# Three products of rounded halves for four readouts, output work shared with two more engines, and new orders on every queue

## The reference

```python
xn = layernorm(x)
scores = einsum('bsd,bmd->bsm', xn, ctx) / sqrt(256)
scores = where(mask, scores, -1e30)
x = x + where(any(mask), softmax(scores) @ ctx, 0)
y = layernorm(x)
h = square(relu(quant_act(y) @ quant_weight(w1).T))      # 8-bit rows, ternary weights
out = x + quant_act(h) @ quant_weight(w2).T
# quant_act: row scaled by 127/max|row| (max at least 1e-5), rounded, scaled back
# quant_weight: gamma = mean|w| + 1e-5; clip(round(w/gamma), -1, 1) * gamma
```

## Time and profile before

| | us |
|---|---|
| median of 3 runs | 66.76 |
| runs | 65.42, 67.02, 66.76 |
| the profiled execution, own time | 65.26 |
| its span, first to last instruction | 63.5 |
| TensorE busy | 59.2 (93%) |
| VectorE, ScalarE, GpSimd busy | 46.3, 46.0, 35.9 |

### The profile page before, as it was taken

The page is one execution under the profiler, slowest core; times in us unless marked ns, Lnnn a source line. Parts: engine busy times, 40 slices in busy tenths (PEclk is TensorE's granted clock), DMA queues, the critical chain, the costliest instruction groups (busy, mean ns, idle before and its releaser), DMA issues.

```text
span 63.5 us, 1281 instructions
## 1 busy us (share of the span) xinstructions
PE 59.2 (93%) x345; PEld 44.0 (69%) x345; DVE 46.3 (73%) x158; ACT 46.0 (72%) x89; POOL 35.9 (57%) x91
## 2 busy tenths in 40 slices
PE   5999999999999999999999999999999799989930
PEld 1337589499898888888958767858687285769710
DVE  0335463995379783595978989899799999999540
ACT  1624937999979799999995693889795799760300
POOL 4340319459002897685738988883898776840000
PEclk9999999999999999999999999999999999999999
DMA  0899999999200010188021647926482718222522
GB/s 0 218 329 312 361 372 401 408 399 404 101 0 0 10 40 7 24 164 148 5 41 41 127 80 151 168 40 134 96 165 51 155 45 163 88 83 83 170 82 88
DMA packets 15024, 9.13 MB, mean 144 GB/s; under 512 B 11557, under 2 KB 13865, under 8 KB 15017
## 3 DMA queue, kind: packets, MB, share of 16 engines
q1 hardware_dynamic: 15008, 9.05, 53.6%
q10 hardware_dynamic: 8, 0.00, 0.0%
HBM read 5.24 MB, written 1.05 MB: 99 GB/s over the span
## 4 chain that ended last, share of the span: by engine, by line
PE 89%; POOL 2%; DVE 2%; issue 1%; ACT 1%; DVEq 0%; POOLq 0%
PE ps_v L389 22%; PE ps_sp L368 13%; PE ps_h L419 9%; PE ps_o L459 6%; PE ps_sp L378 6%; PE ps_h L291 5%; PE ps_h L305 3%; PE ps_sp L350 3%; PE ps_v L459 3%; PE ps_h L368 3%; PE ps_o L327 2%; POOL q L1145 2%; PE ps_sp L419 2%; PE ps_sp L297 2%; PE ps_in L340 1%; PE ps_in L327 1%
## 5 line engine op out<-in xcount | busy, mean ns | idle before, releaser
L389 PE MATMUL ps_v<-ctx_sb,probs_T 128*128 128x256 f32 x64 | 15.3, 383 | 0.0
L389 PEld LDWEIGHTS ps_v<-ctx_sb,probs_T 128*128 128x128 f32 x64 | 11.7, 190 | 2.2 <-issue 0.3
L859 DVE TENSOR_SCALAR_CACHE_REDUCE hidden<-ps_h 128x1024 f32<-128x1024 f32 x6 | 7.3, 1215 | 0.4 <-PE ps_h L419 0.3
L419 PE MATMUL ps_h<-w_T,q_T 128*128 128x512 bf16 x28 | 7.2, 380 | 0.0
L808 DVE CUSTOM_DVE_ANT_0 neg_s<-ps_sp,mask_bias 128x512 f32<-128x512 f32 x7 | 4.8, 689 | 3.0 <-PE ps_sp L368 2.3
L1061 POOL TENSOR_SCALAR ln_ve<-ln_mv 128x2 f32<-128x2 f32 (+1 forms) x5 | 1.0, 194 | 10.1 <-DVE ln_mv L770 10.1
L629 ACT ACTIVATE dev<-x,x_sum 128x256 f32<-128x256 f32 x8 | 4.0, 503 | 3.2 <-DVE x L820 3.2
L616 ACT ACTIVATE probs<-neg_s,neg_max 128x513 f32<-128x513 f32 x8 | 5.7, 716 | 0.3 <-DVE neg_max L808 0.3
L649 ACT ACTIVATE q_i<-hidden,qscale 128x1024 int16<-128x1024 f32 x5 | 5.7, 1138 | 0.0
L368 PE MATMUL ps_sp<-ctx_T_hi,xn_T_hi 128*128 128x512 f32 x12 | 5.3, 444 | 0.0
L820 DVE SCALAR_TENSOR_TENSOR x<-ps_v,recip_sum,x_sb 128x256 f32<-128x256 f32 x8 | 3.9, 482 | 2.0 <-PE ps_v L389 1.9
(11 more groups left out here) (136 smaller groups left out, 147.1 us busy)
## 6 DMA issues: line engine op xcount, KB each, us to landing
ctx_sb<-in_ctx_dram SPq DMA_DIRECT2D x4, 512.0 KB, 7.2
w_sb<-in_L_ffn_w_dram SPq DMA_DIRECT2D x2, 512.0 KB, 6.9
w_sb<-in_L_ffn_w_dram SPq DMA_DIRECT2D x1, 1024.0 KB, 8.5
out_dram<-x_sb SPq DMA_DIRECT2D x8, 128.0 KB, 1.7
x_sb<-in_x_dram SPq DMA_DIRECT2D x3, 256.0 KB, 7.5
x_sb<-in_x_dram SPq DMA_DIRECT2D x2, 128.0 KB, 3.0
q_Ti<-q_i SPq DMA_TRANSPOSE x11, 3.0
w_T<-w_int SPq DMA_TRANSPOSE x4, 3.3
```

The lines of the kernel that those rows point to most:

```text
L389: last = nc.tensor.matmul(ps_v[:, 0:D], probs_T[:, t % 2, c * P:(c + 1) * P], ctx_sb[:, t // TB, c, :], start=(c == 0), stop=(c == MC - 1))
L419: last = nc.tensor.matmul(h_bank(t)[:, n * FH:(n + 1) * FH], q1_T[:, t, dc, :], w1_T[:, n * (FC // 2):(n + 1) * (FC // 2), dc, :], start=( ...
L859: nc.vector.tensor_scalar(hidden[:, t % 3], h_bank(t)[:, :], 0.0, 0.0, ALU.min, ALU.min, accum_out=hidden_min[:, t:t + 1]).then_inc(hidden ...
```

## The change

- Tiles 2 to 5 (batches 1 and 2): `readout` becomes `readout_high` (8 matmuls: rounded probabilities by rounded context, rounded probabilities by context remainder) and `readout_low` (4 matmuls: remainder of the probabilities by rounded context), all float32r, 256 columns, with the next tile's `prob_transposes` between the two. `ctx_rows_high` (ScalarE, one instruction of 128x1024 for each batch) and `ctx_rows_low` (GpSimd, the same size) make the context's halves; `probs_low` (VectorE, 128x512 from PSUM, four times) makes the remainder of the probabilities.
- `weight_integers` moves from GpSimd to VectorE; `cast_q2` of tiles 0 to 2 moves from VectorE to GpSimd; the output step of tiles 0 to 4 is split into a scaling copy on ScalarE (`output_scaled`) and an addition on GpSimd (`output_added`).
- The mask's spread contracts 128 rows of which 124 are zero, where it had four; a memset on VectorE clears them.
- The order of the calls is new on every engine. The number of constant products in the middle is ten, where it was eight.

```diff
+
+HALVED = (1, 3)
+
+CAST = 3
+
...
+        pick = sbuf("pick", [P, B, P], bf16)
+        mask_rows = sbuf("mask_rows", [P, M], bf16)
         mask_bias = sbuf("mask_bias", [P, B, M], f32)
 
...
+        ctx_lo = sbuf("ctx_lo", [P, HALVED[1] - HALVED[0], MC, D], f32r)
         x1 = sbuf("x1", [P, T, D], f32)
 
         x1_sum = sbuf("x1_sum", [P, T], f32)
...
@@ -153,6 +164,7 @@
         ctx_in = [sem(f"ctx_in{b}") for b in range(B)]
...
                 sp.wait_ge(q2i_done, t + 1)
-                if t >= 2:
-                    sp.wait_ge(q2_cast, t - 1)
+                if 2 <= t < CAST + 2:
+                    sp.wait_ge(q2_cast_pool, t - 1)
+                elif t >= 2:
+                    sp.wait_ge(q2_cast, t - 1 - CAST)
                 sp.dma_start_transpose(q2_Ti[:, t % 2], q2_i[:, t % 2]).then_inc(q2_turned[t % 2], 16)
 
             def store(t):
                 b, i = divmod(t, TB)
-                sp.wait_ge(out_ready, t + 1)
+                if t < SHARED:
+                    sp.wait_ge(out_added, t + 1)
+                else:
+                    sp.wait_ge(out_ready, t - SHARED + 1)
...
@@ -259,22 +280,22 @@
             load_ctx(2)
             load_x(3)
             load_ctx(3)
+            turn_weight(0, 0)
             turn_q1(0)
-            turn_weight(0, 0)
             turn_weight(0, 1)
             turn_q1(1)
             turn_q1(2)
+            turn_q2(0)
+            turn_q1(3)
             turn_weight(1, 0)
-            turn_q1(3)
+            turn_q2(1)
+            turn_q1(4)
             turn_weight(1, 1)
-            turn_q2(0)
-            turn_q1(4)
-            turn_q2(1)
             turn_q1(5)
             turn_q2(2)
             turn_q2(3)
+            turn_q2(4)
             store(0)
-            turn_q2(4)
             store(1)
             store(2)
...
                     pe.wait_ge(bias_done, 2)
+                elif halved(t - 1):
+                    pe.wait_ge(plo_done, t - TB * HALVED[0])
                 else:
...
+                last.then_inc(v_done, 1)
+
+            def readout_high(t):
+                b = t // TB - HALVED[0]
+                pe.wait_ge(p_copied, t + 1)
+                pe.wait_ge(ctxlo_done, b + 1)
+                pe.wait_ge(x1_done, t)
+                for part in (ctx_hi, ctx_lo):
+                    for c in range(MC):
+                        nc.tensor.matmul(ps_v[:, 0:D], probs_T_hi[:, t % 2, c * P:(c + 1) * P], part[:, b, c, :],
+                                         start=(part is ctx_hi and c == 0), stop=False)
+
+            def readout_low(t):
+                pe.wait_ge(plo_done, t - TB * HALVED[0] + 1)
+                for c in range(MC):
+                    last = nc.tensor.matmul(ps_v[:, 0:D], probs_T_lo[:, t % 2, c * P:(c + 1) * P],
+                                            ctx_hi[:, t // TB - HALVED[0], c, :], start=False, stop=(c == MC - 1))
                 last.then_inc(v_done, 1)
...
-                if t < TURNED:
-                    pe.wait_ge(q2_cast, t + 1)
+                if t < CAST:
+                    pe.wait_ge(q2_cast_pool, t + 1)
+                elif t < TURNED:
+                    pe.wait_ge(q2_cast, t + 1 - CAST)
                 else:
...
+                elif t - 2 < SHARED:
+                    pe.wait_ge(o_scaled, t - 1)
                 else:
-                    pe.wait_ge(out_ready, t - 1)
+                    pe.wait_ge(out_ready, t - 2 - SHARED + 1)
...
             first_scores(1)
             ctx_transposes(1, 1)
             scores(1)
+            warm_up(ps_q, 128, 4)
             prob_transposes(0)
             x_transposes(1)
-            warm_up(ps_q, 128, 5)
+            warm_up(ps_q, 128, 3)
             weight_sum(0)
             warm_up(ps_q, 128, 3)
             readout(0)
             scores(2)
             ctx_transposes(2, 0)
+            x_transposes(2)
+            prob_transposes(1)
             ctx_transposes(2, 1)
-            prob_transposes(1)
+            scores(3)
+            readout(1)
+            prob_transposes(2)
+            ctx_transposes(3, 0)
+            scores(4)
             weight_sum(1)
-            scores(3)
-            x_transposes(2)
-            prob_transposes(2)
-            readout(1)
-            ctx_transposes(3, 0)
+            readout_high(2)
             prob_transposes(3)
-            scores(4)
+            readout_low(2)
             ctx_transposes(3, 1)
-            readout(2)
+            scores(5)
             x_transposes(3)
-            scores(5)
+            hidden_product(0)
+            readout_high(3)
             prob_transposes(4)
-            readout(3)
-            hidden_product(0)
-            readout(4)
+            readout_low(3)
+            scores(6)
+            readout_high(4)
             prob_transposes(5)
-            scores(6)
+            readout_low(4)
             hidden_product(1)
-            readout(5)
+            readout_high(5)
+            prob_transposes(6)
+            readout_low(5)
+            scores(7)
             hidden_product(2)
-            prob_transposes(6)
-            scores(7)
-            hidden_product(3)
             readout(6)
             prob_transposes(7)
+            hidden_product(3)
+            readout(7)
             hidden_product(4)
-            readout(7)
+            q1_transposes(6)
             output_product(0)
             hidden_product(5)
-            q1_transposes(6)
             hidden_product(6)
+            q1_transposes(7)
             output_product(1)
-            q1_transposes(7)
+            hidden_product_half(0)
             output_product(2)
-            hidden_product_half(0)
             hidden_product_half(1)
+            output_product(3)
             q2_transposes(5)
-            output_product(3)
+            output_product(4)
             q2_transposes(6)
-            output_product(4)
             output_product(5)
             q2_transposes_half(0)
             output_product(6)
...
+            def ctx_rows_high(b):
+                act.wait_ge(ctx_in[b], 16)
+                nc.scalar.activation(ctx_hi[:, b - HALVED[0]], ctx_sb[:, b], ACT.Copy).then_inc(ctxhi_done, 1)
+
...
-                nc.scalar.activation(probs_T[:, t % 2], ps_p, ACT.Copy).then_inc(p_copied, 1)
+                nc.scalar.activation((probs_T_hi if halved(t) else probs_T)[:, t % 2], ps_p, ACT.Copy).then_inc(p_copied, 1)
...
+
+            def output_scaled(t):
+                act.wait_ge(o_done, t + 1)
+                act.wait_ge(oscale_done, t + 1)
+                nc.scalar.activation(x_sb[:, t], o_bank(t), ACT.Copy, scale=oscale[:, t:t + 1]).then_inc(o_scaled, 1)
...
             load_mask()
             mask_copy(0)
             mask_copy(1)
+            mask_copy(2)
             first_ctx_copy(0)
-            mask_copy(2)
             mask_copy(3)
             first_ctx_copy(1)
+            ctx_rows_high(1)
             ctx_high(1, 0)
             weight_abs_sum(0, 0)
             ctx_high(1, 1)
@@ -688,59 +747,65 @@
             weight_abs_sum(0, 1)
             probs_copy(0)
             x_high(1)
+            softmax_exp(1)
+            weight_round(0, 0)
+            weight_round(0, 1)
+            deviation(0)
+            deviation_squares(0)
+            ctx_high(2, 0)
...
-            deviation(6)
             square_to_integers(3)
             deviation(7)
             deviation_squares(7)
             q1_copy(6)
+            output_scaled(0)
             square_to_integers(4)
+            q1_copy(7)
             square(5)
-            q1_copy(7)
+            output_scaled(1)
             square(6)
+            output_scaled(2)
+            output_scaled(3)
             square_half(0)
             q2_copy(5)
+            output_scaled(4)
             square_half(1)
             q2_copy_first_half()
...
+            def zero_mask_rows():
+                nc.vector.memset(mask_rows[:, :], 0.0).then_inc(rows_zero, 1)
+
             def make_pick():
                 dve.wait_ge(ident_done, 1)
-                nc.vector.tensor_copy(pick[:, :, :], ident[0:B, 0:B].unsqueeze(2).broadcast_to([B, B, P])).then_inc(pick_done, 1)
+                nc.vector.tensor_copy(pick[:, :, :], ident[:, 0:B].unsqueeze(2).broadcast_to([P, B, P])).then_inc(pick_done, 1)
...
+            def probs_low(t):
+                dve.wait_ge(p_copied, t + 1)
+                if t - 2 >= TB * HALVED[0]:
+                    dve.wait_ge(v_done, t - 1)
+                nc.vector.tensor_tensor(probs_T_lo[:, t % 2], ps_p, probs_T_hi[:, t % 2], ALU.subtract).then_inc(plo_done, 1)
...
+            def weight_integers(w, half):
+                dve.wait_ge(wround_done, 2 * w + half + 1)
+                nc.vector.tensor_scalar(weight_half(w, half, "int"), weight_half(w, half, "round"), 1.0, -1.0,
+                                        ALU.min, ALU.max).then_inc(wint_done, 1)
...
+            fill_columns()
+            set_ones()
+            zero_mask_rows()
             make_pick()
```

(98 more changed lines are left out.)

155 lines of the change are left out of this document (77 added, 78 removed).

## The result

The changed kernel takes 66.47 us (median of 6 runs, 65.90 to 67.16), beside 66.25 us for the kernel before on the same chip (6 runs, 65.42 to 67.02). The six runs of before fall into two groups, near 65.6 and near 66.9, so beside the ratio of these medians (1.003) stand that on record, which leaves slower executions out (1.022, with a 95% interval of 1.014 to 1.031), and that of the medians of the five lower runs of the changed kernel and the three lower ones of before (66.39 and 65.62), 1.012. So the change costs about 1 to 2%, where 62.5 us was forecast. The profiled execution takes 66.55 us with a span of 64.8; that of before took 65.26.

The account below looks back on a forecast made before the run. TensorE, busy 93% of the span, was taken to bound the kernel until 49.7 us, with waits for GpSimd's quantising later. From the profiled 65.26 us, -1.15 + 0.4 - 1.5 + 0.1 + 0.6 - 1.2 = -2.75 gives 62.5, range 60.9 to 65.9.

Parts of the forecast that it names:

- readouts and their preparation, (b): Tiles 2 to 5: twelve float32r matmuls at 0.12 us gain 1.15 us; preparing the halves costs 0.4.
- start, with two more constant products, (a): Up to `scores(2)`: 128 mask rows raise TensorE's clock near 5.2 us, gaining 1.5; two more constant products cost 0.1.
- waits of helpers, (c): Middle: TensorE waits for work moved between engines, GpSimd's casts above all; 0.6 us charged, bounds 0 and 3.
- the end, (d): Last tiles: output products moved ahead of `q2_transposes(5)` and `(6)` fill waits for GpSimd's quantising; gain 1.2 us, bounds 0 and 1.8.
- stores behind the last output, (e): Kernel's end: stores of tiles 1 to 4 wait for GpSimd's additions, ending near 2 us before the last output; cost nothing.
- the first context's second four transposes: Start, sign that the forecast is right: these transposes at 0.44 us in the chain and not 1.04.
- the level rises no earlier: Rival at the start: TensorE's clock gains nothing from 128 mask rows; 64.0 to 65.5 us, middle 64.6, chance 0.27.
- w2 is then whole near 41: SyncE's queue: w2's transfers, moved behind `turn_q2(0)` and `turn_q2(1)`, are complete near 41 us, first used at 45; cost nothing.
- My worry over `cast_q1(5)`: GpSimd, middle: this cast, behind two `cast_q2` and an inverse deviation, is done within 0.1 us of when `hidden_product(5)` wants it.
- a helper becomes the bound: Rival in the middle: GpSimd's cast or VectorE's `probs_low` comes late, 3 us of waits; 65.5 us, chance 0.15.
- The rival of slow float32r matmuls: Readouts: 256-column matmuls cost 0.235 us each, 2.8 a tile, +4.4 for four; 68.0 us, chance 0.08.
- Preparation at 0.4: Readouts of tiles 2 to 5: making the halves on the helpers makes TensorE wait 0.1 us each; bound 2.

Follow-up runs that it names:

- e7: Changed kernel without GpSimd's residual additions for tiles 1 to 4 (output incomplete there): 64.85 us, ratio 0.983 to the kernel before.
- e10: Changed kernel with the output steps of tiles 2 to 4 back on VectorE: 66.29 us, ratio 1.006 to the kernel before.
- e1: Changed kernel with the stores of tiles 5, 6 and 7 issued from ScalarE's queue: 66.17 us, ratio 1.009 to the kernel before.
- e5: Changed kernel with the mask products contracting 4 rows again: 67.27 us, beside 65.97 for the kernel before.
- e6: Kernel before with only the mask products spread over 128 rows: 65.15 us, ratio 0.988 to the kernel before.
- e2: Changed kernel, on SyncE w2's halves turned ahead of `turn_q1(3)` and `turn_q1(4)`, `turn_q2(1)` behind them: 66.77 us, ratio 1.014 to the kernel before.
- e8: Changed kernel with `cast_q1(5)` directly behind `cast_q1(4)` on GpSimd, ahead of `cast_q2(1)`: 68.35 us, ratio 1.038 to the kernel before.
- e9: Changed kernel with `cast_q1(5)` directly behind `cast_q1(4)` on GpSimd and w2's first half ahead of `turn_q1(3)` on SyncE: 67.91 us, ratio 1.031.
- e12: Changed kernel with `cast_q2` of tiles 0 to 2 back on VectorE: 66.98 us, ratio 1.016 to the kernel before.
- e14: Changed kernel, `cast_q2` of tiles 0 to 2 and outputs of tiles 2 to 4 on VectorE, w2's first half ahead of `turn_q1(3)`: 65.31 us, ratio 1.002.
- e4: Changed kernel with readouts of tiles 2 to 5 as eight float32 matmuls again, without the halves' preparation: 66.89 us, ratio 1.021 to the kernel before.
- e15: Kernel before with the 128-row mask and the three-product readouts with their preparation, old queue order: 66.66 us, ratio 1.016 to the kernel before.
- e3: Changed kernel with the edits of e1 and e2 together: 67.52 us, ratio 1.024 to the kernel before.

## Why the prediction was wrong, step by step

The forecast's terms beside the pieces (a) to (e) of the two profiled executions:

| step | forecast | found |
|---|---|---|
| readouts and their preparation, (b) | -1.15 + 0.4 = -0.75 | -0.77 |
| start, with two more constant products, (a) | -1.5 + 0.1 = -1.4 | -0.10 |
| waits of helpers, (c) | +0.6 | +1.61 |
| the end, (d) | -1.2 | -0.80 |
| stores behind the last output, (e) | 0 | +1.36 |
| sum | -2.75 | +1.30 |

Three steps failed: the stores, the start and the waits of helpers.

**Stores, put at nothing: 1.36 lost, the largest single failure.** I forecast that GpSimd's additions end near 2 us before the last output and "cost nothing while that holds". The last ends at 59.95, 0.8 us before that output starts. The step had weighed only whether they end ahead of it, and not what their late stores do to the last store: the seven stores behind the first, once spread over 8 us, start within 5.3. e7 and e10 bring the time behind the last output back to 2.2 and 2.3 us. e1 shows that a free queue for the last stores gives back 0.2 of it, the rest passing in the landing. That the stores share the transfer engines is the likeliest cause, argued from this and not shown by itself; no run shows them full there.

**The start at -1.5: 0.10 was had.** The mechanism of the level is right: the first context's second four transposes ran at the upper level, as the prediction had asked, and e5 and e6 say that the 128 rows do it. What was wrong is the path from there on. I walked the queues as if `scores(2)` followed TensorE's pace; it follows the landing of w1, 5.67 us behind the first sum of weights, with ScalarE idle ahead of it (0.65 us here). That sum starts at 10.47, and before it started at 10.35, without a wait: there the transfer had just come in time, so next to nothing was left to gain. `softmax_exp(0)` starts at 12.00, where I had 10.9. I named this wait in the step and still took 1.5. The rival "the level rises no earlier" is out as a mechanism, though its time, 64.6, was nearer. The Trainium skill's rule ("TensorE: Matmul & The Clock Gate", "PE-mode transpose") that transposes don't count as busy time in the same way is not decided here: in e5 the ten float32 transposes between 5.12 and 8.0 us change nothing in the pace, but neither do the four score products from 8.03 to 9.74.

**Waits of helpers at +0.6: 1.6, and the step's SyncE part failed.** "w2 is then whole near 41" was wrong: its second half was issued at 44.83 and landed at 48.2. I had walked SyncE's queue by what each transfer waits for and not by its issues, 1.2 to 1.9 us each, of which six stand one behind the other from 38.9 to 47.4. My worry over `cast_q1(5)` was right in place, and 1 us too small, since `cast_q1(4)` ahead of it came late from SyncE. The rival "a helper becomes the bound" is what happened. It is a ring of three queues: e2, e8 and e9 each free one and pay in the next, e12 moves the wait to VectorE, and only e14, which relieves GpSimd and fills SyncE's hole, gets the 1.1 us.

**The end at -1.2: 0.8.** The two waits ahead of the second transposes, 1.07 us in all before, did go: in the chain `q2_transposes(5)` follows `output_product(3)` without one. But the quantising of tile 6 on GpSimd, which carries the late casts, ends at 56.53 and before at 55.94, where I had counted on it some 1 us earlier.

**Readouts: priced right, not collected.** 12 x 0.12 = 1.44 a tile was forecast. The chain of the changed kernel has 1.06 + 0.48, 0.94 + 0.48, 0.95 + 0.48 and 1.05 + 0.48, 1.42 to 1.54. Load records are again 188 to 191 ns and overlap. By the Trainium skill ("TensorE: Matmul & The Clock Gate", section "LDWEIGHTS") 0.107 to 0.11 a matmul would follow as an estimate; the 0.118 to 0.128 of these rows decides. The rival of slow float32r matmuls is out. TensorE's lead at 44 us from this part was 0.77, near the -1.15 + 0.4 of the sum. But e4 shows that the wait at 46.4 takes all but 0.2 of it, and e15 that in the old order the preparation costs more than it brings.

**Preparation at 0.4: the right size for TensorE's waits up to 44 us, and the wrong question.** I priced only TensorE's waits and not what the preparation does to the helpers' queues. `ctx_rows_low` took 2.40 us each, over my upper bound of 2.1 (the estimate of 2.25 from the Trainium skill, "GPSIMD Engine Reference", section 3.1, was the nearer one), and `probs_low` 0.69 each. VectorE had 1.9 us free in the stretch from 30 to 49.4; two of the four `probs_low`, 1.4 us, and two clips of 0.41 fall into it. Its `quantise1(3)` is then what SyncE stands behind from 36.7 to 38.9.

**What stays open.** How the gains of e6 and e14 add up: e14's queues with the old order of the start weren't tried, and the wait for w1 would bound that start too. Whether an earlier transfer of w1 would let the higher level pay was not tried either. Differences under 0.3 us between sets of runs carry no weight: before itself has 65.53 and 65.97 in two sets on one chip.

## What to carry to other kernels

When one engine is at 93% and you give its work to helpers at 75 to 90%, walk each in-order queue by its own instruction times, the DMA issues of SyncE too: work saved on the full engine is worth only what the helpers' next due results allow. Before you price a faster start, look for the transfer that it will have to wait for. Price the last stores as a group; an output finished late on a slow helper delays the one that ends the kernel, even if it has nothing to do with it. Try the free parts of a change alone: here one edit of the mask brought 0.8 us between the medians, and the whole change lost it. And when you set two traces side by side, take off first what their starts differ by.

## What the runs showed of the hardware

- Contracting 128 rows, 124 of them zero, in place of 4 costs nothing in a product (two span 1.06 us with 128 rows, 1.03 with 4, both at the lower level). TensorE's level had risen by 6.7 us in all sixteen traces with 128 rows and rose near 8.8 and 11.9 in the two with 4.
- TensorE's granted clock fell to half after a wait of 2.05 us late in the kernel (e3: 0.5, 0.5 and 0.8 in the slices from 51.15 to 56.1). A wait of 1.07 and one of 1.44 (e9) had no such effect. This is one trace.
- One issue of a store took 1.65 us instead of 0.33 when seven stores started within 5.3 us. With the last three on ScalarE's queue (e1) the last one landed after 2.9 us instead of 1.7.
- A clip of 1024 int16 weights on VectorE was slow beside GpSimd. At 17.95 it took 1.14 us while GpSimd did its two-input subtraction (16.40 to 18.80); in e4, which has no such subtraction, the same clip at 17.83 took 0.40. VectorE's float32 instructions beside the second subtraction (29.05 to 31.44) took their usual 0.68 to 0.69 us.
